# One planner table in a two-layer attention and expert kernel: an expert tile's pieces dealt as gate, up, down instead of laced

## The reference

```python
xn = _layernorm(x)
# attention: 16 heads of 16 features, rms norm of q and k
attn = softmax(einsum(q, k) * D ** -0.5)
s = einsum(attn, v) @ w_proj.T + b_proj
# 8 experts of 176 hidden features, the best 2 per token, and a shared one of 352
probs = softmax(x @ router_w.T)
topk_w, topk_idx = top_k(probs, 2)
out_e = silu(x @ gate_w[e]) * (x @ up_w[e]) @ down_w[e]      # weighted by combine[:, e]
shared = silu(x @ s_gate_w + s_gate_b) * (x @ s_up_w + s_up_b) @ s_down_w + s_down_b
x = x + s * silu(moe_out + shared)
```

## Time and profile before

| what | value |
|---|---|
| three executions | 1422.53, 1424.27, 1422.53 us; median 1422.53 |
| profiled execution, own time | 1423.79 us |
| its span | 1422.0 us, mean granted clock of TensorE 0.994 |
| busy PE / DVE / ACT / POOL | 1382.4 / 920.4 / 819.5 / 761.4 us |
| joint stage | about 895 to 1422 |
| PE's longest sum of waits in it | L1802 for DVE's L1664: 8.5 us in 13 waits |
| DMA | 165.66 MB, mean 116 GB/s |

### The profile page before, as it was taken

How to read it: one execution, slowest core, us unless ns; L and a number is a source line. 1 busy time by engine, 2 the same in 40 slices (tenths; PEclk the granted TensorE clock), 3 DMA queues, 4 the chain that set the end, 5 groups by cost and what they waited for, 6 DMA issues and landing times. The chain is left out here.

```text
span 1422.0 us, 25921 instructions
## 1 busy us (share of the span) xinstructions
PE 1382.4 (97%) x8989; PEld 1236.0 (87%) x8989; DVE 920.4 (65%) x1785; ACT 819.5 (58%) x2172; POOL 761.4 (54%) x757
## 2 busy tenths in 40 slices
PE   9998999999999999999999999899999999999997
PEld 7887798999889988999899988688889989889896
DVE  6655556665656656666655664677787778777764
ACT  5553445554544555445554453378777687777873
POOL 2651434453534454435455443477668677767764
PEclk9999999999999999999999999899999999999999
DMA  5995322333332344223432433144234242333432
GB/s 194 333 332 186 95 77 83 101 102 88 97 104 76 82 116 116 79 50 104 125 86 78 120 90 134 67 128 140 83 105 120 61 148 83 119 115 94 142 120 89
DMA packets 85682, 165.66 MB, mean 116 GB/s; under 512 B 16720, under 2 KB 27664, under 8 KB 83248
## 3 DMA queue, kind: packets, MB, share of 16 engines
q1 hardware_dynamic: 85552, 163.99, 38.1%
HBM read 99.90 MB, written 22.09 MB: 86 GB/s over the span
## 5 line engine op out<-in xcount | busy, mean ns | idle before, releaser
L765 POOL TENSOR_TENSOR a_pr<-a_pr,a_ri 128x512 f32<-128x512 f32 x128 | 133.2, 1041 | 302.2 <-DVE a_ri L945 301.9
L822 ACT ACTIVATE a_pr<-a_score,a_nb 128x256 f32<-128x256 f32 x256 | 118.8, 469 | 270.5 <-DVE a_nb L937 270.5
L1320 POOL TENSOR_TENSOR l_pr<-l_pr,l_ri 128x512 f32<-128x512 f32 x128 | 133.2, 1041 | 125.0 <-DVE l_ri L1689 124.1
L1447 ACT ACTIVATE l_pr<-l_score,l_nb 128x256 f32<-128x256 f32 x256 | 119.0, 471 | 81.0 <-DVE l_nb L1660 80.2
L55 PE MATMUL a_job<-s_xs,s_wh 128*128 128x512 f32 x384 | 154.9, 403 | 1.1 <-PEq L211 1.1
L56 PE MATMUL a_job<-s_xs,s_wh 128*128 128x512 f32 x384 | 151.4, 394 | 0.0
L57 PE MATMUL a_job<-s_xs,s_wl 128*128 128x512 f32 x384 | 151.0, 393 | 0.0
L937 DVE TENSOR_REDUCE a_nb<-a_score 128x2 f32<-128x512 f32 x128 | 88.5, 691 | 89.9 <-PE a_score L1016 89.9
L1660 DVE TENSOR_REDUCE l_nb<-l_score 128x2 f32<-128x512 f32 x128 | 87.6, 684 | 38.0 <-PE l_score L1792 37.4
L950 DVE TENSOR_TENSOR a_pt<-a_turn,a_pt 128x512 fp32r<-128x512 f32 x128 | 87.5, 684 | 23.8 <-ACT a_pt L830 23.8
L1816 PE MATMUL l_out<-s_wh,l_vp 128*128 128x256 f32 x512 | 92.5, 303 | 0.9 <-DVE s_wh L1664 0.9
(11 more groups left out here) (257 smaller groups left out, 4827.5 us busy)
## 6 DMA issues: line engine op xcount, KB each, us to landing
s_wl<-wgu_scratch SPq DMA_DIRECT2D x56, 512.0 KB, 4.7
a_sk<-a_rotk SPq DMA_DIRECT2D x384, 64.0 KB, 2.0
a_sq<-a_rotq SPq DMA_DIRECT2D x256, 64.0 KB, 2.0
s_xs<-xn_scratch SPq DMA_DIRECT2D x14, 1024.0 KB, 5.7
l_wd<-wd_scratch SPq DMA_DIRECT2D x56, 256.0 KB, 2.8
a_raw<-in_w SPq DMA_DIRECT2D x30, 256.0 KB, 2.9
wgu_scratch<-f_split SPq DMA_DIRECT2D x14, 512.0 KB, 4.8
f_praw<-in_moe_w SPq DMA_DIRECT2D x14, 384.0 KB, 4.4
```

Source lines behind the costliest of these rows:

```text
L765: pool.tensor_tensor(e, e, ri[:, n % 2, :].unsqueeze(2).broadcast_to([P, 2, SEQ]), ALU.mult)\
L822: i = act.activation(pr[:, n % 2, t, :], PS[n % 2][:, t * SEQ:(t + 1) * SEQ], ACT.Exp, bias=nb[:, n % 2, t:t + 1], accum_out=sm[:, n % 2, ...
L1320: pool.tensor_tensor(e, e, ri[:, n % 3, :].unsqueeze(2).broadcast_to([P, 2, SEQ]), ALU.mult)\
L1447: i = act.activation(pr[:, n % 3, t, :], PS[n % NPS][:, t * SEQ:(t + 1) * SEQ], ACT.Exp, bias=nb[:, n % 3, t:t + 1], accum_out=sm[:, n % 3 ...
```

## The change

One line of the planner, L1101: the list of pieces.

```diff
-    PIECES = [x for K in range(L + 2) for x in (("g", K), ("G", K), ("D0", K - 2), ("u", K), ("U", K), ("D1", K - 2))
+    PIECES = [x for K in range(L + 2) for x in (("g", K), ("G", K), ("u", K), ("U", K), ("D0", K - 2), ("D1", K - 2))
               if x[1] >= 0 and not (K >= L and x[1] == K)]
```

## The result

The changed kernel took **1430.14 us** (median of 6, 1428.8 to 1434.1) against 1422.76 of the kernel before (median of 6): a ratio of 1.0055, interval 1.0043 to 1.0067. It is 7.4 us slower; the forecast was 1422.2 in a range of 1419.5 to 1426.0. The profiled execution took 1434.1 us, the longest of the six and 4.0 above their median, so differences read from its trace can be larger than those of the medians. One execution of one experiment (before_all) ran at a granted clock of 0.751 and took 1684.9 us; the figures of that kernel are of its nine others.

The account below looks back on a forecast made before the run. The prediction took PE's stream of matmuls to bound the joint stage, with only 11.9 us of idle time and low-clock stretches movable. Gains of 2.1 less losses of 1.75 gave -0.35 and 1422.2 us, range 1419.5 to 1426.0.

Parts of the forecast that it names:

- (e): Head: DVE's product now ahead of the first max delays exps, scores and the first gate tile: +0.6 us.
- (d): Two small gains, slots unnamed, where a job waits for a bank whose earlier user is now earlier: -0.2 us each.
- (g): Four slots with a long DVE job (scale_rows or slow k_lo) beside the moved product: +0.55 us in all.
- (a): Slots 104 and 105: D0 of tile 42 no longer waits for y_sum, but the next chain limits the gain: -0.5 us.
- (b): Slots 71 to 75: U of tile 30 and POOL's pair leave the slot, easing hid_hi and transpose waits: -0.7 us.
- (c): Slots 112 to 114, tiles 47 and 48: ACT's hid_hi wait for POOL's combine eases, transposes come earlier: -0.54 us.
- (f): Slot 87: U's product now stands between DVE's reciprocal and max, so L1664 and the transposes are late: +0.6 us.
- The signs: Checks on the after-profile; wrong if L1802's L1664 waits left 8.5 by over 3 us, clock differed, or time left range.
- Rival 1: Joint stage slower: DVE is full where U lands, L1578 exposed in ten slots, +4.5 us, 1427.0; chance 0.14.
- Rival 3: The clock moves: one more half-clock stretch +1.5 us, both gone -3, so 1419.2 to 1423.7; chance 0.16.
- Rival 2: Faster: the stalls touched vanish and nothing takes their place, 3.3 us gained, no loss, 1419.2; chance 0.08.

Follow-up runs that it names:

- before_all: Kernel before, with DVE's reciprocal ahead of a U that opens a slot and the second half deferred from its first G or U: 1425.05 us, ratio 1.0017.
- followers_later: Changed kernel, with POOL's combine and hid_lo and ACT's hid_hi of tile 3 one slot later, as before; PE and DVE order kept: 1428.36 us.
- only_tile3: Kernel before, with the pieces of tile 3 alone dealt in the order of the change: 1427.3 us, ratio 1.0038.
- recip_first: On tile3_laced, DVE's reciprocal put ahead of U's product where U is the slot's first item: 1425.15 us, ratio 1.0030.
- tile3_laced: Changed kernel, with the six pieces of tile 3 alone dealt laced as before: 1426.25 us, ratio 1.0023.
- laced3_defer_u: On tile3_laced, a slot's last U product on DVE put behind the next slot's max and L1664: 1435.73 us, ratio 1.0089.
- laced3_all: On tile3_laced, reciprocal ahead of a U that opens a slot, second half deferred from its first G or U: 1429.28 us, ratio 1.0043.

## Why the prediction was wrong

**Step (e) failed.** It read the head on DVE and priced what DVE's new order costs, +0.6; followers_later, where that order is left, shows 0.72. But the step took the list of DVE alone, though the sentence ahead of the sum had named the combine among what moves a slot earlier. POOL's list was not followed at this place: that the combine of the first routed tile waits for a load whose issue hangs on SyncE's order (unchanged, so no earlier), and that pow and normalise are queued behind it. No row of before showed a wait there, because the combine came just after the landing. The real price was 6.0 us in the trace of the changed kernel, 5.1 in that of only_tile3, and 3.9 to 4.8 in the medians.

**The other steps**, by the slots. The prediction named no slots for (d) and (g); those in the table are the ones whose change fits their words, found afterwards.

| step | foretold | measured in the traces |
|---|---|---|
| (a) slots 104, 105 | -0.5 | -0.53, and +0.26 in 103 |
| (b) slots 71 to 75 | -0.7 | -0.70 |
| (c) slots 112 to 114 | -0.54 | -0.56 |
| (d) slot 49 / 106 to 108 | -0.2 / -0.2 | +0.97 / -0.22 |
| (e) head | +0.6 | +6.04 |
| (f) slots 87, 88 | +0.6 | +0.72 |
| (g) four slots | +0.55 | slots 40 to 42 +0.80, 90 +0.56, 109 and 110 +1.12 |

In (a) the wait for y_sum went and the next chain took over, as foretold; the rows of the changed kernel are on ACT and PE:

```profile
1332.13 1.14 ACT L1475 ACTIVATE l_yt<-l_y 128x512 f32<-128x512 f32 x2
1333.18 0.59 ACT L1455 ACTIVATE s_wh<-l_turn 128x512 fp32r<-128x512 f32 x1
...
1334.64 0.63 PE L1802 MATMUL l_turn<-s_ident,l_pr 128*128 128x128 f32 x4 [0.55 <-DVE s_wh L1664]
```

(c) missed that U of tiles 46 and 47, each a slot earlier, come into slots 108 and 110; slots 109 and 110 pay 1.12. (d) had the sign wrong at slot 49: the bank's earlier user U came earlier on PE but behind the norm on DVE, and Q's product waits. (f) was right, one slot later than named:

```profile
1271.00 0.69 DVE L1578 TENSOR_TENSOR l_ga<-l_ga,l_job 128x512 f32<-128x512 f32 x1
1271.61 0.68 DVE L1660 TENSOR_REDUCE l_nb<-l_score 128x2 f32<-128x512 f32 x1
1272.21 0.68 DVE L1664 TENSOR_TENSOR s_wh<-l_turn,s_wh 128x512 fp32r<-128x512 f32 x1
```

(g) was too small, 0.55 against 2.5: a U's product ahead of the reciprocal or of the next max, with POOL and ACT carrying it on. The mechanism is shown at slots 40 to 42 (recip_first); at 90 and 110 it is argued only. Outside the head the sum was foretold at -0.95 and measured at +3.7 in the medians (tile3_laced). The traces of before and tile3_laced, with half clock behind the same two logits jobs, differ by 3.9 from slot 3 on; the rows of the slot table make up 2.7 of it (slots 3 to 19 left aside), and the rest, 1.3, lies in slots 4, 7, 51 to 55 and 65, which no experiment looked at. One count was wrong too: D0 changes its slot in 37 tiles, not only in the 21 whose U moves, and once by three slots.

The signs came out mixed. The waits of L1802 for L1664 stayed within 3 us of 8.5 (11.1). The granted clock did differ in the two stretches: 1.00 at 1134.50 behind the job of slot 52, and none low behind that of slot 84. ACT's waits for POOL's combine were to shrink and grew, from 2.6 to 8.5 us.

**The rivals.** Rival 1 (DVE is full where U lands) was foretold at 1427.0 and is the nearest to the number, by the wrong road: its mechanism is shown for some 1.5 us (slots 40 to 42 and 88), may hold for 1.7 more (90, 109, 110), and the largest single loss is POOL's wait. Rival 3 named the clock and priced a stretch at 1.5 us; slots 20 and 21 show 1.3. The head's stretch at half clock followed a wait that the change made, at a place it had not named. Rival 2 is refuted.

## What to carry to other kernels

When a producer moves a slot earlier, follow every engine that acts behind it, and ask of each what else it waits for. A consumer that came just after a DMA's landing shows no wait at all; one slot earlier it blocked its whole queue here, for 2.95 us. And of two products that wait on another engine, the one that has few readers may be put behind the critical work of the next slot (G here: -4.5 us); the one with a chain behind it may not (U here: +9.5 on tile3_laced).

## What was not expected of the hardware

PE at half clock: with the wait of 3.08 us ahead of 940.45 the granted clock was 0.51 from 939.60 to 946.40. In only_tile3, with 3.09 us of waiting ahead of 938.32, it was 0.50 from 939.70 to 943.00. In laced3_defer_u it was 0.51 from 1170.90 on, with the wait of 2.32 ahead of 1171.36. These are the only waits of PE over 2 us in the main part of the joint stage of the traces kept; those of 1.1 to 1.74 us had no such stretch behind them. But a long wait isn't needed: in laced3_all a stretch at 0.50 at 1170.00 came behind two waits of 0.90 and 0.85. What the clock costs shows in the head behind the wait: that part is 2.8 us longer than before in the changed kernel, with 6.8 us at half clock, and 1.6 us longer in only_tile3, with 3.4. In followers_later, with 1.12 us at the head, the mean behind 930 was 1.00:

```profile
930.00:1403.00 473.00, 457.04 (x3183) 411.89 (x3182) 351.03 (x740) 361.37 (x1059) 344.17 (x420) 1.00 0.37 113
```

In slots 20, 21 and 84, 85, behind the logits jobs, such a stretch of 3.4 us costs 1.3 us, and it comes in some traces and not in others, also where the order of the pieces there is the same: in the changed kernel after the job at slot 20 (0.50 at 1014.80) and not after the others, in the kernel before after those at slots 52 and 84. The Trainium skill, TensorE: Matmul & The Clock Gate, section What's actually happening, says that the activity check runs freely and isn't aligned to the program; these places agree with it, but no run here isolates it.

scale_rows L1592 in slot 55 took 1.22 us before the change and 2.01 with it, where POOL ran hid_lo and a spread beside it, with U of tile 24 two slots earlier (the first row is of before, the two others of the changed kernel):

```profile
1134.55 1.22 DVE L1592 TENSOR_TENSOR l_qk<-l_qk,l_rq 128x1024 f32<-128x1024 f32 x1
...
1144.63 1.28 POOL L1331 TENSOR_TENSOR l_hid<-l_ga,l_hid 128x512 fp32r<-128x512 f32 x1
...
1144.99 2.01 DVE L1592 TENSOR_TENSOR l_qk<-l_qk,l_rq 128x1024 f32<-128x1024 f32 x1
```

The Trainium skill, GPSIMD Engine Reference, section Key points, has GpSimd and VectorE share SBUF interfaces; the trace agrees, in scale_rows (2.01 and 1.22 us) and in L135 of the head (0.99 us beside the normalise, 0.15 before), and this is one way in which a step moved on POOL makes DVE late.
